# Turning neighbour means two blocks per q unit, and expert products in two PSUM banks: a graph layer with attention and routed experts

## The chip, the cores and the metric

The kernel runs on one core of a Trainium2 chip. The metric is the time of one execution on the device in microseconds (us). The kernel before takes 750.01 us, the median of 3 runs (749.41 to 750.44).

## What is computed

One layer of a graph transformer over 1,250 nodes of 512 values and 40,000 edges, sorted by destination. The three parts, cut to their core:

```python
xn = layernorm(x)
# graph part: mean of the neighbours' rows, two products, norm, relu
agg = segment_sum(xn[src], dst) / max(count(dst), 1)
gnn = relu(layernorm(xn @ w_self.T + agg @ w_neigh.T + bias) * gamma + beta)
# linear attention: 8 heads of 64, phi(t) = elu(t @ proj_mat) + 1
q, k, v = split(xn @ w_qkv)
kv = sum_n phi(k)[n] (x) v[n];  z = 1 / (phi(q) . sum_n phi(k)[n])
mix = (phi(q) @ kv * z) @ w_proj + b_proj
x = x + gnn + mix
# feed-forward: a shared hidden layer, and 2 of 8 experts per node
y = layernorm(x) * ln_scale + ln_bias
out = swiglu(y @ shared_in.T) @ shared_out.T + shared_out_b
h = swiglu(y @ expert_in.T)                  # one hidden row for all experts
for e in range(8): out += comb[:, e] * (h @ expert_out[e].T) + cnt[:, e] * bias[e]
return x + out
```

## The kernel before, in words

Each engine has a program of its own in `build`, written out in the order in which it is to run; semaphores (`S[...]`) tie the engines together. No scheduler moves anything: an instruction that waits holds up all that stands behind it on its engine. Every product of f32 values is made of three f16 products (high x high, high x low, low x high), in the helper `split3` (its matmul is L1343, so nearly all products carry that line). For a transposed operand this means: PE transposes a block into a PSUM bank, ACT copies it out as f16 (the high half), and DVE subtracts the high half from the bank and keeps the rest (the low half).

The change touches two stages.

**The q stage.** The sums of the neighbours lie in `aggacc`, ten blocks of 125 nodes. DVE makes means of them (L1029, one instruction per block, semaphore `an_rdy`). For each block, `means_T` then stands on three engines: PE transposes it (four matmuls, L1544, `aT_mm`), into bank 6 or 7 by turns, ACT writes the high half (L574, `aT_h`), DVE the low half (L1033, `aT_rdy`). PE may use the bank again when the low half of the block two before is made (L1542). Between the blocks PE makes the twelve q units: four pairs of heads for each of three groups of nodes (4, 4 and 2 tiles of 125 nodes), twelve matmuls each, in the banks `qb`. For each unit ACT makes two relus and an exponential (L585, L586, L588), and DVE adds up phi(q) (L1044, `q_rdy`). phi(q) is written to `qphi`, which is the same memory as `aggacc`, so a block has to be transposed before the q unit that writes over it. `MEANS` says which blocks PE turns after which q unit:

```python
MEANS = [(0, 1, 2), (3, 4, 5), (6, 7), (8, 9)] + [()] * 8
```

ACT has blocks 0 to 2 behind its unit 0 and blocks 3 to 9 behind its unit 1. DVE has all ten scalings first, then all ten low halves, and only then phi(q) of unit 0. `unit(U_PROJ)` converts a weight from f32 to two f16 halves: L435 on ACT and L745 on DVE. The attention tiles follow (`att`, L1572; the first of DVE's part at L1058 waits for all twelve `q_rdy`), then `att_turn` (L1581) and `project`.

**The expert stage.** The 2,500 pairs of node and expert are sorted by expert into tiles of 128 rows. GpSimd gathers the hidden rows of a tile (L377), PE turns them with 16 matmuls (`turn`, L1701) into the banks 4 to 7, ACT and DVE copy the turned rows out (L705, L1313; `hg_h`, `hg_l`). `expert` makes the product of a turned tile with the expert's weight, 24 matmuls of 512 columns, all in bank 0. ACT's `result` waits until it is done (`me_mm`) and until the store before has landed (`y_st`), copies bank 0 to `yb` (L710, `y_cp`), and issues the store to `y_rows` (L712). Pass i of PE's loop is: wait for `hg_h`, `hg_l`, `g_rdy`; turn tile i + 1; wait for `y_cp` of product i - 1; product i. Between experts ACT and DVE convert two weights each (`late_units`). Here there are 23 products. After them come ten tiles of the shared output (`so_mm`), in the banks `sobank`, and DVE adds the gathered expert rows and these banks to x (L1327, L1331).

Of the kernel before, what the change touches and what calls it, by code (L numbers as in the profile page):

```python
# [11 lines left out]
ACT = mybir.ActivationFunctionType  # L12
# [48 lines left out]
GROUPS = [(0, 4), (4, 4), (8, 2)]  # L61
MEANS = [(0, 1, 2), (3, 4, 5), (6, 7), (8, 9)] + [()] * 8
PARTS = [(0, 112), (112, P)]
# [27 lines left out]
def build(nc, a, out):  # L91
    with ExitStack() as ctx:
# [152 lines left out]
        kvb = [ps[3], ps[5]]  # L245
        qb = [ps[0], ps[1], ps[2], ps[4]]
        turned = [PS[:, 4 + 2 * z:6 + 2 * z, :].rearrange("p b (j n) -> p (b j) n", n=ST) for z in range(2)]

        sobank = [ps[i] for i in (1, 2, 3, 4, 5, 6, 7, 0)]

# [174 lines left out]
        def _(act):  # L425
# [145 lines left out]

            def means_T(b):
                act.wait_ge(S["aT_mm"], b + 1)
                s.activation(aggT[:, 0, :, b * BLK:(b + 1) * BLK], ps[6 + b % 2][:, 0:C * BLK].rearrange("p (c n) -> p c n", c=C),  # L574
                             ACT.Copy).then_inc(S["aT_h"], 1)
# [3 lines left out]
            for t0, nt in GROUPS:  # L579
                for r in range(PAIRS):  # L580
                    o, w = 1024 * (n % 2), nt * P
                    act.wait_ge(S["q_mm"], n + 1)
                    if n >= 2:
                        act.wait_ge(S["q_rdy"], n - 1)
                    s.activation(mscr[:, o:o + w], qb[n % 4][:, 0:w], ACT.Relu, scale=-1 / WS).then_inc(S["q_neg"], 1)  # L585
                    s.activation(mscr[:, o + 512:o + 512 + w], qb[n % 4][:, 0:w], ACT.Relu, scale=1 / WS).then_inc(S["q_rel"], 1)  # L586
                    act.wait_ge(S["q_neg"], n + 1)
                    s.activation(mscr[:, o:o + w], mscr[:, o:o + w], ACT.Exp, scale=-1.0).then_inc(S["q_exp"], 1)  # L588
                    for b in (range(3), range(3, NBLK))[n] if n < 2 else ():
                        means_T(b)  # L590
                    if n == 4:
                        unit(U_PROJ)
                    n += 1
# [113 lines left out]
            def result(i):  # L707
                act.wait_ge(S["me_mm"], i)
                act.wait_ge(S["y_st"], 16 * i)
                s.activation(yb, ps[0][:, :], ACT.Copy).then_inc(S["y_cp"], 1)  # L710
                act.wait_ge(S["y_cp"], i)
                act.dma_start(y_rows[bass.ds((i - 1) * ST, ST), :], yb).then_inc(S["y_st"], 16)  # L712
# [20 lines left out]
        def _(dve):  # L733
# [293 lines left out]
            link(v.reciprocal(cntacc[:, :], cntacc[:, :]))  # L1027
            for b in range(NBLK):
                v.tensor_scalar(aggacc[0:BLK, b, :], aggacc[0:BLK, b, :], cntacc[:, b:b + 1], None, ALU.mult).then_inc(S["an_rdy"], 1)  # L1029

            def means_T(b):
                dve.wait_ge(S["aT_h"], b + 1)
                v.tensor_tensor(aggT[:, 1, :, b * BLK:(b + 1) * BLK], ps[6 + b % 2][:, 0:C * BLK].rearrange("p (c n) -> p c n", c=C),  # L1033
                                aggT[:, 0, :, b * BLK:(b + 1) * BLK], ALU.subtract).then_inc(S["aT_rdy"], 1)


            for b in range(NBLK):
                means_T(b)
            n = 0
            for t0, nt in GROUPS:  # L1040
                for r in range(PAIRS):
                    o, w = 1024 * (n % 2), nt * P
                    dve.wait_ge(S["q_exp"], n + 1)
                    v.scalar_tensor_tensor(out=qphi[:, r, t0 * P:t0 * P + w], in0=mscr[:, o:o + w], scalar=1.0,  # L1044
                                           in1=mscr[:, o + 512:o + 512 + w], op0=ALU.mult, op1=ALU.add).then_inc(S["q_rdy"], 1)
                    n += 1
                    if n == 5:
                        unit(U_PROJ)
# [287 lines left out]
        def _(pe):  # L1336
# [201 lines left out]

            def means_T(b):
                pe.wait_ge(S["an_rdy"], b + 1)  # L1540
                if b >= 2:
                    pe.wait_ge(S["aT_rdy"], b - 1)  # L1542
                for c in range(C):
                    ins = te.transpose(ps[6 + b % 2][:, c * BLK:(c + 1) * BLK], aggacc[0:BLK, b, c * 128:(c + 1) * 128], ident[0:BLK, 0:BLK])  # L1544
                ins.then_inc(S["aT_mm"], 1)
# [166 lines left out]

            def expert(e, cur):
                split3(ps[0][:, :], lambda s, c: hgT2[:, cur(s * HID + c * 128)], unitv(U_EXP + 2 * e), J, True, True).then_inc(S["me_mm"], 1)

# [5 lines left out]
            pe.wait_ge(S["h_f"], 3 * J)  # L1721
            expert(0, lambda o: slice(o, o + 128))
            for e in range(EXP):
                pe.wait_ge(S["w_rdy"], U_EXP + 2 * e + 2)
                with pe.Fori(1 if e == 0 else ends[e - 1], ends[e]) as i:
# [4 lines left out]
                    turn(lambda o: hg2[:, bass.ds(nx + o, 128)])  # L1730
                    pe.wait_ge(S["y_cp"], i)
                    cur = pe.snap((i % 2) * ROWW)
                    expert(e, lambda o: bass.ds(cur + o, 128))

            pe.wait_ge(S["w_rdy"], U_SOUT + 2)
            pe.wait_ge(S["h_rdy"], 3 * J)
            for t in range(TILES):
                if t == 3:
                    pe.wait_ge(S["hg_h"], total + 1)
                    pe.wait_ge(S["hg_l"], total + 1)  # L1740
                if t == 7:
                    pe.wait_ge(S["y_cp"], total)
# [56 lines left out]
```

## Time and profile before

| | us |
|---|---|
| median of 3 runs | 750.01 (749.41 to 750.44) |
| the profiled execution | 746.69 |
| its span in the trace | 744.7 |
| PE matmuls busy | 708.5 (95%) |
| DVE busy | 386.4 (52%) |
| ACT busy | 261.9 (35%) |
| GpSimd busy | 174.4 (23%) |

The durations in the trace add up to the span; 2.0 us of the profiled execution lie around it. The profiled execution was 3.3 us shorter than the median of the runs. PE is TensorE's matmuls, PEld its weight loads, which run beside matmuls; the end of a matmul is modelled, so rows of matmuls overlap slightly, and a row's start is the more exact number. A name such as PEq or ACTq is the engine's sequencer. "[3.17 <-DVE big L1033]" behind a row of the timeline means that the engine stood idle for 3.17 us just before it and what released it.

### The profile page before, as it was taken

To read this page: it belongs to the slowest core of one execution; us is meant where nothing else is said; L and a number is where in the kernel's file an instruction comes from. 1 tells how busy PE (TensorE), PEld (TensorE's weight loads), DVE (VectorE), ACT (ScalarE), POOL (GpSimd) and SP (SyncE) were. 2 spreads that over 40 slices of the span, in tenths; PEclk is the share of its full clock that TensorE was granted. 3 is DMA by queue.
4 is the path that set the end of the run, shared out by engine and by line. 5 is a ranking of instruction groups with operands and counts; after the bars stand their busy time and mean duration, and the time that the engine had idled before them with its cause. 6 is when DMAs were issued, how large, how long until landed. Compare 5 with 4: busy or idle time off the path is not lost.

```text
span 744.7 us, 12041 instructions
## 1 busy us (share of the span) xinstructions
PE 708.5 (95%) x4382; PEld 433.8 (58%) x4382; DVE 386.4 (52%) x735; ACT 261.9 (35%) x386; POOL 174.4 (23%) x170
## 2 busy tenths in 40 slices
PE   6989899997999999998999999999889999999998
PEld 5646577774576656565756644446745555555554
DVE  5874678964476757876246422222235523441154
ACT  4853123323652231356353123333336443532000
POOL 3340000000061000013222257742312212222362
PEclk9999999998999999999999999999999999999999
DMA  9200002000031150011325212222166766643675
GB/s 249 96 1 1 1 2 114 2 13 2 1 138 61 29 198 1 0 28 28 114 84 169 56 28 58 58 79 92 29 227 239 264 216 239 230 136 130 195 211 150
DMA packets 24417, 73.90 MB, mean 99 GB/s; under 512 B 7059, under 2 KB 7405, under 8 KB 20274
## 3 DMA queue, kind: packets, MB, share of 16 engines
q1 hardware_dynamic: 8607, 39.74, 15.8%
q0 software_dynamic: 10768, 25.52, 11.6%
q10 hardware_dynamic: 4994, 8.01, 2.9%
q8 instruction: 31, 0.51, 0.3%
q14 instruction: 17, 0.13, 0.1%
HBM read 57.90 MB, written 15.31 MB: 98 GB/s over the span
## 4 chain that ended last, share of the span: by engine, by line
PE 77%; DVE 11%; ACT 6%; issue 3%; DMA 3%; DVEq 0%; POOL 0%; SPq 0%; ACTq 0%; POOLq 0%
PE banks L1343 59%; PE banks L1392 6%; PE banks L1380 3%; PE banks L1701 3%; DMA y_rows<-xT 2%; DVE st L768 1%; PE banks L1572 1%; PE banks L1366 1%; ACT W L435 1%; DMA x<-in_x 1%; PE banks L1581 1%; DVE xn L1154 1%; DVE W L745 1%; PE banks L1373 1%; ACT big L612 1%
## 5 line engine op out<-in xcount | busy, mean ns | idle before, releaser
L1343 PE MATMUL banks<-W,xT 128*125 128x512 f16 (+1 forms) x1392 | 318.2, 383 | 8.0 <-ACT xT L710 2.2
L1343 PEld LDWEIGHTS banks<-W,xT 128*125 128x125 f16 (+2 forms) x1392 | 165.3, 122 | 137.4 <-issue 15.9
L1343 PE MATMUL banks<-xT,W 128*128 128x500 f16 (+1 forms) x720 | 131.0, 344 | 1.8 <-DVE xn L1293 1.4
L1343 PEld LDWEIGHTS banks<-xT,W 128*128 128x128 f16 x720 | 70.7, 99 | 60.5 <-issue 4.4
L745 DVE SCALAR_TENSOR_TENSOR W<-stg,W 128x2048 f16<-128x2048 f32 x30 | 68.5, 2304 | 40.9 <-ACT W L435 40.9
L1343 PE MATMUL banks<-W,big 128*125 128x512 f16 x360 | 81.5, 380 | 0.0
L1343 PEld LDWEIGHTS banks<-W,big 128*125 128x125 f16 x360 | 48.3, 136 | 29.2 <-issue 2.3
L377 POOL DMA_INDIRECT xn<-h_rows,tokidx x29 | 35.3, 1217 | 125.1 <-PE banks L1701 114.7
L366 POOL TENSOR_TENSOR big<-xn,big 125x512 f16<-125x512 f32 x20 | 23.5, 1173 | 174.7 <-ACT big L627 174.7
L1313 DVE CAST xT<-banks 128x1024 f32 x22 | 26.9, 1222 | 69.0 <-PE banks L1701 69.0
L435 ACT ACTIVATE W<-stg 128x2048 f16<-128x2048 f32 x30 | 56.4, 1903 | 0.0
L1392 PE MATMUL banks<-W,big 125*125 125x512 f16 x200 | 54.0, 393 | 0.6 <-ACT big L566 0.6
L360 POOL TENSOR_TENSOR x<-x,bproj 125x512 f32<-125x512 f32 x10 | 14.4, 1476 | 165.6 <-DVE big L1044 165.6
L1293 DVE SCALAR_TENSOR_TENSOR xn<-banks,xn 128x500 f32<-128x500 f32 (+1 forms) x24 | 14.2, 591 | 69.8 <-ACT xn L689 69.8
L710 ACT ACTIVATE xT<-banks 128x512 f32<-128x512 f32 x23 | 13.7, 597 | 66.9 <-PE banks L1343 41.5
L390 POOL TENSOR_TENSOR big<-xn,big 128x500 f16<-128x500 f32 (+1 forms) x24 | 22.7, 945 | 45.9 <-ACT big L692 45.9
L689 ACT ACTIVATE xn<-banks 128x500 f32<-128x500 f32 (+1 forms) x24 | 12.4, 516 | 52.8 <-PE banks L1343 47.5
L897 DVE TENSOR_TENSOR W<-big 125x2048 f16<-125x2048 f16 x23 | 28.1, 1223 | 3.3 <-DVE big L893 2.4
L1154 DVE SCALAR_TENSOR_TENSOR xn<-banks,xn 125x512 f32<-125x512 f32 x20 | 13.8, 690 | 30.5 <-ACT xn L623 30.5
L1701 PEld LDWEIGHTS banks<-ident,xn 128*128 (+1 forms) x384 | 24.0, 100 | 8.5 <-issue 1.8
L1701 PE MATMUL banks<-ident,xn 128*128 128x128 f16 x384 | 26.2, 223 | 2.9 <-POOLq L382 1.5
L420 POOL DMA_INDIRECT xT<-y_rows,sloti x20 | 24.7, 1236 | 16.1 <-issue 9.3
(324 smaller groups left out, 785.0 us busy)
## 6 DMA issues: line engine op xcount, KB each, us to landing
stg<-in_units SPq DMA_DIRECT2D x30, 1024.0 KB
y_rows<-xT ACTq DMA_DIRECT2D x29, 256.0 KB
h_rows<-big POOLq DMA_DIRECT2D x10, 500.0 KB, 3.6
out_x<-x SPq DMA_DIRECT2D x10, 224.0 KB
stg<-in_wqkT SPq DMA_DIRECT2D x2, 1024.0 KB, 11.0
x<-in_x SPq DMA_DIRECT2D x2, 896.0 KB
xn<-h_rows,tokidx POOLq DMA_INDIRECT x29, 5.3
x<-in_x SPq DMA_DIRECT2D x1, 448.0 KB
```

The costliest lines, as they stand in the source:

```text
L366: g.tensor_tensor(hrow[t % 2][:, HID + 512 * u:HID + 512 * (u + 1)], mscr[0:P, 1024 + 512 * u:1536 + 512 * u], hrow[t % 2][:, 512 * u:512 ...
L377: g.indirect_dma_start(hg[i % 2], None, h_rows, bass.IndirectOffsetOnAxis(ap=tokidx[:, i:i + 1], axis=0)).then_inc(g_in[i % 2], 16)
L390: g.tensor_tensor(hT[:, 1, j, c0:c0 + w], mscr[:, 1024 + 512 * (n % 2):1024 + 512 * (n % 2) + w], hT[:, 0, j, c0:c0 + w], ALU.subtract).th ...
L420: g.indirect_dma_start(yg[n % 4], None, y_rows, bass.IndirectOffsetOnAxis(ap=sloti[:, 0, k, t:t + 1], axis=0)).then_inc(yg_in[n % 4], 16)
L435: s.activation(W[:, u % NSLOT, 0, :], stg[:, u % NSTG, :], ACT.Copy, scale=WS).then_inc(S["w_h"], 1)
L745: v.scalar_tensor_tensor(out=W[:, u % NSLOT, 1, :], in0=stg[:, u % NSTG, :], scalar=WS, in1=W[:, u % NSLOT, 0, :], op0=ALU.mult, op1=ALU.s ...
L897: return v.tensor_tensor(ohw[g % RING], iotaP.unsqueeze(1).to_broadcast(every), kr[g % KRING].rearrange("p k (a b) -> p (k a) b", b=2).uns ...
L1313: v.tensor_copy(hgT[:, bass.ds((i + 1) % 2, 1), 1].rearrange("p z j n -> p (z j) n"), turned[1]).then_inc(S["hg_l"], 1)
L1343: ins = te.matmul(dst, lhs(sl, c), rhs(sr, c), start=(first and c == 0 and k == 0), stop=(last and c == n - 1 and k == 2))
L1380: ins = te.matmul(ps[q][:, o:o + WK], ohw[z][:, CH // 2 + k // 2, :, k % 2], ohw[z][:, k // 2, 0:WK, k % 2], start=(h == 0 and k == 0), st ...
L1392: ins = te.matmul(ps[4 + z][0:BLK, :], CT[z][0:P, t, :], xs[:, s, t, :], start=(t == 0 and s == 0), stop=(t == TILES - 1 and s == 1))
L1701: ins = te.matmul(turned[s][:, j, :], rows(s * HID + j * 128), ident16[:, :], start=True, stop=True)
```

## The change

`MEANS` now gives each of the q units 0 to 4 two blocks, on PE, ACT and DVE alike. DVE scales four blocks first, and two more behind the low halves of each of the units 0, 1 and 2. `TURN_OF` is the order of the blocks (position p takes block `TURN_OF[p]`), such that each is turned before phi(q) is written over it. The conversion of `U_PROJ` stands behind q unit 6 on ACT and DVE, where it stood behind unit 4. The product of pass i goes to bank i % 2, by a register in the matmul's destination; PE no longer waits for `y_cp` in the loop; ACT reads bank (i + 1) % 2. `sobank` begins with bank 2, and the waits of the shared output move with it.

```diff
-MEANS = [(0, 1, 2), (3, 4, 5), (6, 7), (8, 9)] + [()] * 8
+MEANS = [(0, 1), (2, 3), (4, 5), (6, 7), (8, 9)] + [()] * 7
+TURN_OF = [0, 1, 2, 3, 4, 5, 7, 8, 6, 9]
...
+        PSflat = PS.rearrange("p b n -> p (b n)")
-        sobank = [ps[i] for i in (1, 2, 3, 4, 5, 6, 7, 0)]
+        sobank = [ps[i] for i in (2, 3, 4, 5, 6, 7, 0, 1)]
...
-            def means_T(b):
-                act.wait_ge(S["aT_mm"], b + 1)
-                s.activation(aggT[:, 0, :, b * BLK:(b + 1) * BLK], ps[6 + b % 2][:, 0:C * BLK].rearrange("p (c n) -> p c n", c=C),
+            def means_T(p):
+                b = TURN_OF[p]
+                act.wait_ge(S["aT_mm"], p + 1)
+                s.activation(aggT[:, 0, :, b * BLK:(b + 1) * BLK], ps[6 + p % 2][:, 0:C * BLK].rearrange("p (c n) -> p c n", c=C),
                              ACT.Copy).then_inc(S["aT_h"], 1)
...
-                    for b in (range(3), range(3, NBLK))[n] if n < 2 else ():
+                    for b in MEANS[n]:
                         means_T(b)
-                    if n == 4:
+                    if n == 6:
                         unit(U_PROJ)
...
-                s.activation(yb, ps[0][:, :], ACT.Copy).then_inc(S["y_cp"], 1)
+                s.activation(yb.unsqueeze(1), PS[:, bass.ds((i + 1) % 2, 1), :], ACT.Copy).then_inc(S["y_cp"], 1)
...
-            for b in range(NBLK):
+            def scale_mean(p):
+                b = TURN_OF[p]
                 v.tensor_scalar(aggacc[0:BLK, b, :], aggacc[0:BLK, b, :], cntacc[:, b:b + 1], None, ALU.mult).then_inc(S["an_rdy"], 1)
...
-            for b in range(NBLK):
-                means_T(b)
+            for b in range(4):
+                scale_mean(b)
             n = 0
             for t0, nt in GROUPS:
                 for r in range(PAIRS):
                     o, w = 1024 * (n % 2), nt * P
+                    for b in MEANS[n]:
+                        means_T(b)
+                    for b in MEANS[n + 2] if n < 3 else ():
+                        scale_mean(b)
                     dve.wait_ge(S["q_exp"], n + 1)
...
-                    if n == 5:
+                    if n == 7:
                         unit(U_PROJ)
...
-            def means_T(b):
-                pe.wait_ge(S["an_rdy"], b + 1)
-                if b >= 2:
-                    pe.wait_ge(S["aT_rdy"], b - 1)
+            def means_T(p):
+                b = TURN_OF[p]
+                pe.wait_ge(S["an_rdy"], p + 1)
+                if p >= 2:
+                    pe.wait_ge(S["aT_rdy"], p - 1)
                 for c in range(C):
-                    ins = te.transpose(ps[6 + b % 2][:, c * BLK:(c + 1) * BLK], aggacc[0:BLK, b, c * 128:(c + 1) * 128], ident[0:BLK, 0:BLK])
+                    ins = te.transpose(ps[6 + p % 2][:, c * BLK:(c + 1) * BLK], aggacc[0:BLK, b, c * 128:(c + 1) * 128], ident[0:BLK, 0:BLK])
...
-            def expert(e, cur):
-                split3(ps[0][:, :], lambda s, c: hgT2[:, cur(s * HID + c * 128)], unitv(U_EXP + 2 * e), J, True, True).then_inc(S["me_mm"], 1)
+            def expert(e, cur, bank):
+                split3(bank, lambda s, c: hgT2[:, cur(s * HID + c * 128)], unitv(U_EXP + 2 * e), J, True, True).then_inc(S["me_mm"], 1)
...
                     turn(lambda o: hg2[:, bass.ds(nx + o, 128)])
-                    pe.wait_ge(S["y_cp"], i)
                     cur = pe.snap((i % 2) * ROWW)
-                    expert(e, lambda o: bass.ds(cur + o, 128))
+                    bank = pe.snap((i % 2) * 512)
+                    expert(e, lambda o: bass.ds(cur + o, 128), PSflat[:, bass.ds(bank, 512)])
...
             for t in range(TILES):
-                if t == 3:
+                if t == 2:
                     pe.wait_ge(S["hg_h"], total + 1)
                     pe.wait_ge(S["hg_l"], total + 1)
-                if t == 7:
+                if t == 6:
                     pe.wait_ge(S["y_cp"], total)
```

The same at the places of the prediction, in the order of each engine. The low halves are the rows `big<-banks,big`, the scalings `big<-big,etabs`, phi(q) is `big<-xn`. DVE before, from the scalings on:

```order
L1029 TENSOR_SCALAR big<-big,etabs 125x512 [waits dve_ch]
L1029 TENSOR_SCALAR big<-big,etabs 125x512 x9
L1033 TENSOR_TENSOR big<-banks,big 128x4x125 [waits aT_h] x10
L1044 SCALAR_TENSOR_TENSOR big<-xn 128x500 [waits q_exp] x2
L1051 COPY kvbd<-banks 128x260 [waits kvacc_mm]
L1044 SCALAR_TENSOR_TENSOR big<-xn 128x500 [waits q_exp] x3
L745 SCALAR_TENSOR_TENSOR W<-stg,W 128x2048 [waits w_h]
```

DVE of the change, the same stretch up to unit 2:

```order
L1033 TENSOR_SCALAR big<-big,etabs 125x512 [waits dve_ch]
L1033 TENSOR_SCALAR big<-big,etabs 125x512 x3
L1038 TENSOR_TENSOR big<-banks,big 128x4x125 [waits aT_h] x2
L1033 TENSOR_SCALAR big<-big,etabs 125x512 x2
L1053 SCALAR_TENSOR_TENSOR big<-xn 128x500 [waits q_exp]
L1038 TENSOR_TENSOR big<-banks,big 128x4x125 [waits aT_h] x2
L1033 TENSOR_SCALAR big<-big,etabs 125x512 x2
L1053 SCALAR_TENSOR_TENSOR big<-xn 128x500 [waits q_exp]
L1060 COPY kvbd<-banks 128x260 [waits kvacc_mm]
```

The first low half stands behind four scalings where it stood behind ten, and phi(q) of unit 0 behind two low halves where it stood behind ten.

PE before, at the start of a pass's product in the expert loop (`banks<-ident,xn` is the turn, `banks<-W,xT` the product, ISA a register operation):

```order
L1701 ISA
L1701 MATMUL banks<-ident,xn 128x128
L1343 ISA [waits y_cp]
L1343 MATMUL banks<-W,xT 128x512 x2
L1343 ISA
L1343 MATMUL banks<-W,xT 128x512
```

PE of the change, the same place:

```order
L1711 ISA
L1711 MATMUL banks<-ident,xn 128x128
L1352 ISA
L1352 REGISTER_ALU
L1352 MATMUL banks<-W,xT 128x512 x2
L1352 ISA
L1352 MATMUL banks<-W,xT 128x512
```

The wait is gone, and one register operation per product is new, for the bank; the number of ISA rows between the matmuls is the same.

## Rows read from the trace of the kernel before

**Rows 1.** The page, part 1: busy time, share of the span, instructions.

```profile
PE 708.5 (95%) x4382; PEld 433.8 (58%) x4382; DVE 386.4 (52%) x735; ACT 261.9 (35%) x386; POOL 174.4 (23%) x170
```

**Rows 2.** Timeline of DVE in the tail: start, us, line, operation, count, [idle before <-releaser].

```profile
738.53 0.75 DVE L1327 SCALAR_TENSOR_TENSOR x<-xT,wch,x 125x512 f32<-125x512 f32 x1 [1.58 <-DMA xT<-y_rows,sloti]
741.28 0.69 DVE L1331 SCALAR_TENSOR_TENSOR x<-banks,x 125x512 f32<-125x512 f32 x1 [2.00 <-PE banks L1343]
```

**Rows 3.** Timeline of PE in the q stage (columns as in rows 2).

```profile
172.87 1.07 PE L1544 MATMUL banks<-ident,big 125*128 125x125 f32 x8 [0.22 <-DVE big L1029]
177.12 0.62 PE L1544 MATMUL banks<-ident,big 125*128 125x125 f32 x4 [3.17 <-DVE big L1033]
177.57 4.38 PE L1343 MATMUL banks<-xT,W 128*128 128x500 f16 x12
...
184.89 1.07 PE L1544 MATMUL banks<-ident,big 125*128 125x125 f32 x4 [2.09 <-DVE big L1033]
...
190.39 2.70 PE L1343 MATMUL banks<-xT,W 128*128 128x500 f16 x12
192.93 1.02 PE L1544 MATMUL banks<-ident,big 125*128 125x125 f32 x8
193.78 15.42 PE L1343 MATMUL banks<-xT,W 128*128 128x500 f16 x96
209.13 2.13 PE L1572 MATMUL banks<-kvbd,big 64*125 64x65 f32 x32
```

**Rows 4.** Stretches: length; busy us PE, PEld, DVE, ACT, POOL; granted clock; DMA share, GB/s.

```profile
172.80:177.10 4.30, 1.07 (x8) 0.86 (x9) 4.30 (x12) 2.42 (x5) 0.00 (x0) 1.00 0.01 2
177.10:182.00 4.90, 4.88 (x18) 2.33 (x19) 1.13 (x2) 0.61 (x2) 0.00 (x0) 0.65 0.00 0
```

**Rows 5.** Timeline of DVE in the q stage.

```profile
172.33 4.05 DVE L1029 TENSOR_SCALAR big<-big,etabs 125x512 f32<-125x512 f32 x10
176.30 1.25 DVE L1033 TENSOR_TENSOR big<-banks,big 128x500 f16<-128x500 f32 x2
...
210.46 0.42 DVE L1044 SCALAR_TENSOR_TENSOR big<-xn 128x250 f32<-128x250 f32 x1 [0.41 <-ACT xn L588]
```

**Rows 6.** Timeline of ACT in the q stage.

```profile
172.69 0.59 ACT L585 ACTIVATE xn<-banks 128x500 f32<-128x500 f32 x1 [7.77 <-PE banks L1343]
...
174.15 1.07 ACT L574 ACTIVATE big<-banks 128x500 f16<-128x500 f32 x2
```

**Rows 7.** Timeline of PE in the expert stage.

```profile
545.44 5.35 PE L1343 MATMUL banks<-W,xT 128*128 128x512 f16 x24
...
553.53 5.35 PE L1343 MATMUL banks<-W,xT 128*128 128x512 f16 x24 [1.85 <-ACT xT L710]
558.72 1.06 PE L1701 MATMUL banks<-ident,xn 128*128 128x128 f16 x16
559.79 5.35 PE L1343 MATMUL banks<-W,xT 128*128 128x512 f16 x24
...
679.02 5.35 PE L1343 MATMUL banks<-W,xT 128*128 128x512 f16 x24
```

**Rows 8.** Timeline of ACT and PE's weight loads in one pass of the expert loop.

```profile
559.01 0.60 ACT L710 ACTIVATE xT<-banks 128x512 f32<-128x512 f32 x1 [3.85 <-PE banks L1343]
559.78 4.86 PEld L1343 LDWEIGHTS banks<-W,xT 128*128 x24 [0.18 <-issue]
...
560.37 1.02 ACT L705 ACTIVATE xT<-banks 128x1024 f32 x1 [0.77 <-PE banks L1701]
561.29 3.70 ACT L435 ACTIVATE W<-stg 128x2048 f16<-128x2048 f32 x2
```

**Rows 9.** Timeline of ACT at the last product of the loop.

```profile
678.24 0.60 ACT L710 ACTIVATE xT<-banks 128x512 f32<-128x512 f32 x1 [3.87 <-PE banks L1343]
```

**Rows 10.** What ACT's copy of the product (L710) waited for: us, times.

```profile
  DMA y_rows<-xT: 25.3, 6
```

**Rows 11.** Register operations of the turn (L1701) on PE's sequencer: ns, starts.

```profile
L1701 PEldq FUSED_REGOPS  x352: 46/46/128, 540.9 to 677.4; - x176
```

More of the change, by code:

```diff
@@ L1027, in _ @@
             link(v.reciprocal(cntacc[:, :], cntacc[:, :]))
-            for b in range(NBLK):
+            def scale_mean(p):
+                b = TURN_OF[p]
                 v.tensor_scalar(aggacc[0:BLK, b, :], aggacc[0:BLK, b, :], cntacc[:, b:b + 1], None, ALU.mult).then_inc(S["an_rdy"], 1)
-            def means_T(b):
-                dve.wait_ge(S["aT_h"], b + 1)
-                v.tensor_tensor(aggT[:, 1, :, b * BLK:(b + 1) * BLK], ps[6 + b % 2][:, 0:C * BLK].rearrange("p (c n) -> p c n", c=C),
+            def means_T(p):
+                b = TURN_OF[p]
+                dve.wait_ge(S["aT_h"], p + 1)
+                v.tensor_tensor(aggT[:, 1, :, b * BLK:(b + 1) * BLK], ps[6 + p % 2][:, 0:C * BLK].rearrange("p (c n) -> p c n", c=C),
                                 aggT[:, 0, :, b * BLK:(b + 1) * BLK], ALU.subtract).then_inc(S["aT_rdy"], 1)
-            for b in range(NBLK):
-                means_T(b)
+            for b in range(4):
+                scale_mean(b)
             n = 0
@@ L1537, in _, with means_T @@
                 ins.then_inc(S["x_mm"], 1)
-            def means_T(b):
-                pe.wait_ge(S["an_rdy"], b + 1)
-                if b >= 2:
-                    pe.wait_ge(S["aT_rdy"], b - 1)
+            def means_T(p):
+                b = TURN_OF[p]
+                pe.wait_ge(S["an_rdy"], p + 1)
+                if p >= 2:
+                    pe.wait_ge(S["aT_rdy"], p - 1)
                 for c in range(C):
-                    ins = te.transpose(ps[6 + b % 2][:, c * BLK:(c + 1) * BLK], aggacc[0:BLK, b, c * 128:(c + 1) * 128], ident[0:BLK, 0:BLK])
+                    ins = te.transpose(ps[6 + p % 2][:, c * BLK:(c + 1) * BLK], aggacc[0:BLK, b, c * 128:(c + 1) * 128], ident[0:BLK, 0:BLK])
                 ins.then_inc(S["aT_mm"], 1)
@@ L1721, in _ @@
             pe.wait_ge(S["h_f"], 3 * J)
-            expert(0, lambda o: slice(o, o + 128))
+            expert(0, lambda o: slice(o, o + 128), ps[0][:, :])
             for e in range(EXP):
```

## The prediction

> **What bounds the kernel now.** The page's busy times come first: PE is busy 95% of the span, DVE 52%, ACT 35% [rows 1]. So an edit pays where PE stands still or runs slowly, or not at all. Next is the end of the kernel: DVE's last addition waits 2.00 us for PE's last tile, while the last gathered row was added 2.0 us before (738.53 + 0.75 against 741.28) [rows 2]. The end hangs on PE, and every us that PE wins earlier reaches it, as long as no other engine had less to spare.
>
> Then I looked in PE's timeline for places where it is not at full pace. In the q stage it waits 3.17 us and 2.09 us for DVE's low halves (L1033) [rows 3]. Both waits have a second price. The unit behind the first takes 4.38 us, the same twelve matmuls later take 2.70 us [rows 3]. The stretches tell why: PE is busy 1.07 of 4.30 us while it waits, and in the next 4.90 us, though it is busy throughout, the granted clock is 0.65 on average, that is partly 1.2 and partly 2.4 GHz [rows 4].
>
> Why the waits? DVE starts its ten scalings at 172.33 and needs 4.05 us for them; the first low half begins at 176.30 [rows 5]. But ACT had the first high half done by 174.15 + 0.59 = 174.74 [rows 6], so DVE came 1.6 us late. PE wants the third block turned before the second q unit, and it can't reuse a bank before that low half is made. Three blocks per unit in two banks make it worse: the third always waits for ACT and DVE.
>
> In the expert stage one wait is plain, 1.85 us at 553.53 [rows 7]. The others hide in the modelled ends of matmuls. Turn and product start at 558.72 and 559.79, 1.07 us apart [rows 7], and the weight loads stood idle for 0.18 us just before the product [rows 8]. ACT's copy of the last product ran from 559.01 to 559.61 [rows 8]; 0.18 us after its end the product starts. So the copy, not the array, sets the start of a product.
>
> **The change, part by part.**
>
> *q stage.* At full pace it needs: five pairs of transposed blocks at 0.85 us (192.93 to 193.78), three units at 2.54 us (190.39 to 192.93), and the last eight units at 15.35 us (193.78 to 209.13) [rows 3]. That is 4.25 + 7.62 + 15.35 = 27.22 us. It took 209.13 - 172.87 = 36.26 us. If nothing makes PE wait, **9.0 us** go: 5.3 us of waits, the rest the slow clock.
>
> Is the cover long enough? After a unit's start come 2.70 us until it ends [rows 3], 1.46 us of relus and exponential (172.69 to 174.15), 0.59 us for the first high half [rows 6], 1.25 us for two low halves [rows 5], and hops between engines, together some 0.2 us: 6.2 us. PE asks for the second of these banks after a unit, a pair, a unit and half a pair: 2.54 + 0.85 + 2.54 + 0.43 = 6.36 us. The margin is some 0.15 us. I take it as held, and note it as thin: a miss of 0.1 us in each of three units would cost 0.3 us and leave PE busy. DVE's own load for a unit is two low halves (1.25), two scalings (0.81), and phi(q), under 0.84 (a half-wide one takes 0.42) [rows 5]: at most 2.9 us in 3.39 us. The first pair of low halves waits for four scalings (1.6 us, to 173.95) and for ACT's 174.74, so the scalings are covered.
>
> The conversion of U_PROJ, now behind unit 6, takes ACT some 1.85 us (two take 3.70 [rows 8]) and is followed by five units, four of half width. Before, DVE's last phi(q) ended at 210.88 [rows 5], 1.75 us behind PE's last unit. By the same durations I get 1.7 to 2.0 us for it now, so the attention stage starts earlier by nearly the whole gain. Weights, bias and GpSimd's additions are released by events that move with it; I cost them at nothing.
>
> *Expert stage.* Without the wait for `y_cp` a pass is product plus turn: 5.19 us (553.53 to 558.72) and 1.07 - 0.18 = 0.89 us [rows 7, 8], 6.08 us in place of 6.26 us. From 545.44 to 679.02 there are 21 passes, 133.58 us; 21 x 6.08 = 127.68 us. With the 0.18 us ahead of the first one, **6.1 us** go: 3.9 us of the short waits and 2.2 us of the long ones.
>
> What takes over the duty of the wait is `hg_h`, which ACT signals behind the copy. In the pass shown it ends at 561.39 [rows 8], and PE wants it at the product's end, 564.98, so ACT has 3.4 us to spare in the shorter pass. The store that lands latest held ACT up by 1.85 us: covered. ACT's copy waited for a store 6 times of 23 [rows 10]; copy and issue take 0.78 us (559.01 to 559.79) [rows 7, 8], so a store may take 5.3 us before it sets the pass, and in the other 17 passes it had landed within 5.5 us. Late ones eat from the 3.4 us, and the next pass gives it back. In passes with two conversions ACT is busy until 564.99 [rows 8] and wanted at 565.07: still enough.
>
> The destination of the 24 matmuls is now in a register. No row prices this. PE's sequencer issues the last turn's register operations at 677.4 [rows 11] and next waits for ACT's copy, done at 678.84 [rows 9], so it is idle for 1.4 us of a pass of 6.26 and works 4.8 us. The lower bound is nothing, the upper one 128 ns per matmul, the longest of its register operations [rows 11]. I take nothing, since the order shows no further operation per matmul. Up to 52 ns per matmul (1.26 / 24) the idle time covers it.
>
> The Trainium skill ("TensorE: Matmul & The Clock Gate", section "Wait — 56ns, not 53.3ns?") says that matmuls are issued to the engine directly, and that through microcode each would take about 62 ns; it doesn't speak of register destinations, and no row here shows either price. By that figure, as an estimate, a pass would need 4.8 + 1.5 = 6.3 us, and the expert stage would give about 1 us.
>
> *Shared output.* The rotated banks move the waits of tiles 3 and 7 to tiles 2 and 6, 11 us or more behind the events that they wait for. Nothing.
>
> Sum: 9.0 + 6.1 = 15.1 us. Against the profiled execution that is 746.7 - 15.1 = 731.6 us; the median of the runs stands 3.3 us above it, so I forecast 750.0 - 15.1 = **734.9 us**.
>
> **The rivals.**
>
> *A. The short gaps are not the wait for the copy.* If the switch from turn to product costs 0.18 us by itself, only the long waits go: 133.58 - 21 x 6.26 = 2.1 us. Then 9.0 + 2.1 = 11.1 us, 738.9 us. Against it: the product follows the end of the copy by 0.18 us also when the copy is late, and the switch from product to turn costs nothing. The Trainium skill ("TensorE: Matmul & The Clock Gate", section "HAM oscillation — how this bites in real kernels") tells of a kernel to which PSUM double-buffering gave no further gain; by that rule A would be the outcome. The 0.18 us of idle weight loads in the row before [rows 8] speak against it, since a wait is there to be removed.
>
> *B. The chain through ACT and DVE is longer than summed.* If one wait of the size of the two stays, and with it the slow clock, half of the 9.0 us is lost: 739.4 us. For it: the thin margin. Against it: each engine's load per unit is below PE's.
>
> *C. Register destinations bind PE's sequencer.* At 128 ns per matmul a pass takes 4.8 + 3.1 = 7.9 us against 6.36 on average now: 21 x 1.5 = 32 us more, less 9.0 us: 773 us, slower than before. It turns the sign from 82 ns per matmul on ((6.36 + 9.0 / 21 - 4.8) / 24). Against it: the turn's weight loads have register addresses too, and run at full pace.
>
> *D. The gain is lost downstream* in a transfer or a chain that starts at a fixed time. I found none behind the q stage; the time would stay at 750 us.
>
> **How the numbers follow.** Forecast 0.75, A 0.12, B 0.07, C 0.04, D 0.02. The forecast's own range is about 732 to 738 us (the profiled execution and the median differ by 3.3 us, and so may two measurements). Up to 740.5 us it takes in A and B; C and D stay outside. A measurement of this kernel can tell about 0.2% (1.5 us) from no change. Faster 0.94, the same 0.02 (D), slower 0.04 (C).
>
> **What would show it.** Right: no wait above 0.3 us before the transposed blocks, a granted clock of 1.00 throughout the q stage, and the attention stage starting 27 us after the first transposition; product starts 6.08 us apart, no idle weight loads before a product, no PE wait for L710. Wrong: passes of 6.26 us (A), a wait for L1033's successor followed by slow units (B), passes above 6.3 us with idle weight loads between the product's matmuls (C), or a new wait of PE on another engine between the stages (D).

## The result and the profile after

The changed kernel takes 736.85 us (median of 4 runs, 735.89 to 738.54), the kernel before 750.23 us (median of 4). The ratio is 0.9852, with a 95% interval of 0.9819 to 0.9884: 13.4 us faster, where 15.1 us were forecast. Beside later runs of the kernel before it is 12.6 us (e5) and 12.4 us (e11). The profiled execution took 737.12 us, its span is 735.3 us. The page, part 1 (answers to [rows 1]):

```profile
PE 705.9 (96%) x4382; PEld 434.2 (59%) x4382; DVE 386.4 (53%) x735; ACT 261.8 (36%) x386; POOL 172.8 (23%) x170
```

Where did the time go? From the starts of the same instructions in both traces:

| stretch | before, us | after, us | difference |
|---|---|---|---|
| start to the first transposed block | 172.87 | 174.53 | +1.66 |
| to the first attention tile | 36.26 | 27.29 | -8.97 |
| to the second expert product | 336.31 | 336.09 | -0.22 |
| its 21 passes, to the last product | 133.58 | 131.67 | -1.91 |
| to the end | 65.68 | 65.72 | +0.04 |
| span | 744.7 | 735.3 | -9.4 |

The first line lies ahead of everything that was changed. Its 1.66 us are the clock, about (0.76 - 0.51) x 7.00 = 1.75 us: busy time in the stretch from 85 to 92 us (length; busy us and count of PE, PEld, DVE, ACT, POOL; granted clock, DMA share, GB/s), after, then before:

```profile
85.00:92.00 7.00, 7.00 (x23) 3.08 (x23) 4.68 (x13) 0.30 (x1) 0.00 (x0) 0.51 0.00 1
```

```profile
85.00:92.00 7.00, 7.00 (x45) 3.83 (x43) 5.26 (x13) 0.60 (x1) 0.00 (x0) 0.76 0.00 1
```

PE was busy all the time in both, at a granted clock of 0.51 and 0.76, with equal programs there. Such a difference is scatter between executions, and one execution cannot be set against another without looking for it.

**The q stage.** PE's timeline after (start, us, line, operation, count; answers to [rows 3]):

```profile
174.53 1.07 PE L1554 MATMUL banks<-ident,big 125*128 125x125 f32 x8 [0.22 <-DVE big L1033]
175.44 2.70 PE L1352 MATMUL banks<-xT,W 128*128 128x500 f16 x12
...
178.83 2.70 PE L1352 MATMUL banks<-xT,W 128*128 128x500 f16 x12
...
189.00 12.88 PE L1352 MATMUL banks<-xT,W 128*128 128x500 f16 x84
201.82 2.30 PE L1582 MATMUL banks<-kvbd,big 64*125 64x65 f32 x32
```

No wait stands behind the first one. A unit and a pair take 3.39 us (175.44 to 178.83), and the attention stage starts 27.29 us after the first transposed block; the forecast had 27.22. The granted clock is 1.00 from 172.80 to 204.00. DVE's timeline (answers to [rows 5]):

```profile
173.99 1.67 DVE L1033 TENSOR_SCALAR big<-big,etabs 125x512 f32<-125x512 f32 x4
176.44 1.26 DVE L1038 TENSOR_TENSOR big<-banks,big 128x500 f16<-128x500 f32 x2 [0.78 <-ACT big L577]
...
203.31 0.42 DVE L1053 SCALAR_TENSOR_TENSOR big<-xn 128x250 f32<-128x250 f32 x1 [0.41 <-ACT xn L591]
```

The scalings end at 175.66; the low half then waits 0.78 us for ACT, so the scalings are off the path. DVE's last phi(q) ends at 203.73, 1.9 us behind the start of attention; before it was 1.75 us.

**The expert stage.** PE's timeline (answers to [rows 7]):

```profile
537.91 5.34 PE L1352 MATMUL banks<-W,xT 128*128 128x512 f16 x24
543.09 1.06 PE L1711 MATMUL banks<-ident,xn 128*128 128x128 f16 x16
543.99 5.34 PE L1352 MATMUL banks<-W,xT 128*128 128x512 f16 x24
...
550.21 5.34 PE L1352 MATMUL banks<-W,xT 128*128 128x512 f16 x24
...
574.96 5.34 PE L1352 MATMUL banks<-W,xT 128*128 128x512 f16 x24
580.35 2.27 PE L1711 MATMUL banks<-ident,xn 128*128 128x128 f16 x16
582.67 5.34 PE L1352 MATMUL banks<-W,xT 128*128 128x512 f16 x24
587.91 2.16 PE L1711 MATMUL banks<-ident,xn 128*128 128x128 f16 x16
590.12 5.34 PE L1352 MATMUL banks<-W,xT 128*128 128x512 f16 x24
```

The first pass has 6.08 us (537.91 to 543.99), as forecast, with no gap between turn and product. But 543.99 to 550.21 is 6.22, and 574.96 to 582.67 is 7.71: the 16 matmuls of that turn took 2.27 us in place of 1.06 (both with 0.2 us of modelled end, so 0.13 to 0.14 us from start to start in place of 0.056 us). The next turn is nearly as slow, with 2.16 us. It isn't the clock, as the stretch around the first slow turn shows (columns as above):

```profile
577.50:584.30 6.80, 6.70 (x37) 3.41 (x36) 2.42 (x2) 5.71 (x5) 1.42 (x1) 1.00 0.38 135
```

Behind the first slow turn stands ACT:

```profile
569.67 0.34 ACTq L715 DMA_DIRECT2D y_rows<-xT  x1
...
577.69 0.60 ACT L713 ACTIVATE xT<-banks 128x512 f32 x1 [6.45 <-DMA y_rows<-xT]
...
579.02 1.02 ACT L708 ACTIVATE xT<-banks 128x1024 f32 x1 [0.73 <-ACT xT L713]
579.94 3.70 ACT L437 ACTIVATE W<-stg 128x2048 f16<-128x2048 f32 x2
```

The store issued at 569.67 held the next copy up until 577.69, 8.0 us later: ACT stood idle for 6.45 us. Not all of this is delay: in an undisturbed pass the copy starts 0.44 us behind the turn (601.81 and 601.37), here that would be 574.28, so it is 3.4 us late. The high half is done at 580.04, and the turn starts at 580.35. The second slow turn has DVE behind it, whose cast (`hg_l`) stands behind two conversions, which stand behind ACT's late ones:

```profile
581.88 4.49 DVE L748 SCALAR_TENSOR_TENSOR W<-stg,W 128x2048 f16<-128x2048 f32 x2 [5.53 <-ACT W L437]
586.29 1.22 DVE L1322 CAST xT<-banks 128x1024 f32 x1
```

The cast ends at 587.51, the turn starts at 587.91. What the copy waited for in all (answers to [rows 10]):

```profile
  DMA y_rows<-xT: 41.9, 12
  PE banks L1352: 23.2, 7
```

ACT stood idle until a store landed 12 times, before 6 times, and for 41.9 us in place of 25.3. These sums overstate the delay: ACT also idles some 3.6 us ahead of a copy that is on time, and in e4 below, where no copy waits for a store by itself, the same row reads 43.2 us in 10 times. The starts say more: counted as above, the copy began over 0.5 us late in 8 of the 22 passes of the loop, before in one.

### The profile page after: what moved, and what is told of

Read it like the earlier page. It is cut to its first block, busy times and chain, and to the rows that moved or that the text cites. A ratio compares the mean times of both kernels' runs of the same rounds, so it can differ in the third digit from the quotient of the medians.

```text
span 735.3 us, 12086 instructions
## 1 busy us (share of the span) xinstructions
PE 705.9 (96%) x4382; PEld 434.2 (59%) x4382; DVE 386.4 (53%) x735; ACT 261.8 (36%) x386; POOL 172.8 (23%) x170
## 4 chain that ended last, share of the span: by engine, by line
PE 82%; DVE 10%; ACT 4%; issue 3%; DMA 1%; DVEq 0%; POOL 0%; SPq 0%; ACTq 0%; POOLq 0%
PE banks L1352 62%; PE banks L1401 7%; PE banks L1711 3%; PE banks L1389 3%; DVE st L771 1%; PE banks L1582 1%; PE banks L1375 1%; DMA x<-in_x 1%; PE banks L1591 1%; ACT W L437 1%; DVE xn L1163 1%; PE banks L1382 1%; PE banks L1554 1%; PE banks L1416 1%; ACT big L615 1%
## 5 line engine op out<-in xcount | busy, mean ns | idle before, releaser
L1352 PE MATMUL banks<-xT,W 128*128 128x500 f16 (+1 forms) x720 | 128.3, 339 | 1.8 <-DVE xn L1302 1.4
L713 ACT ACTIVATE xT<-banks 128x512 f32 x23 | 13.7, 597 | 65.3 <-DMA y_rows<-xT 41.9
L1711 PE MATMUL banks<-ident,xn 128*128 128x128 f16 x384 | 28.6, 224 | 2.9 <-POOLq L384 1.5
L1711 PEld LDWEIGHTS banks<-ident,xn 128*128 (+1 forms) x384 | 25.3, 100 | 10.1 <-issue 2.7
L692 ACT ACTIVATE xn<-banks 128x500 f32<-128x500 f32 (+1 forms) x24 | 12.4, 516 | 52.7 <-PE banks L1352 47.5
L708 ACT ACTIVATE xT<-banks 128x1024 f32 x22 | 22.5, 1024 | 16.6 <-ACT xT L713 9.6
```

The source lines that it names most:

```text
L708: s.activation(hgT[:, bass.ds(i % 2, 1), 0].rearrange("p z j n -> p (z j) n"), turned[0], ACT.Copy).then_inc(S["hg_h"], 1)
L1352: ins = te.matmul(dst, lhs(sl, c), rhs(sr, c), start=(first and c == 0 and k == 0), stop=(last and c == n - 1 and k == 2))
L1711: ins = te.matmul(turned[s][:, j, :], rows(s * HID + j * 128), ident16[:, :], start=True, stop=True)
```

## The experiments

Two theories on the passes that stayed long. **Theory 1:** stores that share the DMA engines with two weight loads land late; ACT's copy, the conversions behind it and DVE's cast come late, and PE's turn is released when it should long have been issued. **Theory 2:** two banks or the register destination make passes long by themselves. Theory 1 leaves out a third signal that the turn waits for: `g_rdy`, that the gathered hidden rows of the next tile have landed. They come by DMA too, and share its engines with the same loads. Beside these: what in the q part counts, and what the medians have that the profiles don't. "Passes" is always the time from the start of the second product to that of the last. The kernel before ran with each group: median 746.99 us (17 runs, 741.64 to 751.71) beside e1 to e4, 748.00 (17 runs) beside e5 to e8, 748.34 (11 runs) beside e9 to e12.

**e1 and e2: each half alone.** e1 is the change without its expert part, e2 the kernel before with the expert part:

```diff
# e1, against the change
-    expert(e, lambda o: bass.ds(cur + o, 128), PSflat[:, bass.ds(bank, 512)])
+    pe.wait_ge(S["y_cp"], i)
+    expert(e, lambda o: bass.ds(cur + o, 128))        # bank 0
# e2, against the kernel before: the same two lines the other way round
```

> The q stage as in the change, the expert stage as before. If the q stage gives what its trace shows (27.3 us from the first transposed block to the attention stage, where it was 36.3), this is 9.0 us faster than before, about 741.2 us, ratio 0.988, and its expert passes are the 6.26 us of before. If part of the q gain is lost later (a fixed transfer, attention that waits), it is 745 us or more.

> The q stage as before, the expert stage as in the change. The forecast's 6.1 us would give 744.1 us. The trace of the change shows only 1.9 us won in the 21 passes, and the medians leave 4.4 us for this half, so I expect 746 to 748 us, with passes of 6.08 us and a few long ones around the weight loads. If the two halves disturb each other, this half alone gives the full 6.1 us.

e1: 736.83 us (6 runs), ratio 0.986 (0.982 to 0.990), 10.2 us faster. q stage 27.29 us, passes 133.70 us. e2: 744.94 us (12 runs), ratio 0.997 (0.9941 to 0.9999), 2.0 us faster. q stage 36.27 us, passes 131.56 us. So the q part makes most of the gain, the halves add up about (12.2 us) to what both give, and the expert part alone gives 2 us, not 6.1. Its ordinary passes are 6.07 us here too. Both came out below the expected times, and so did the kernel before beside them (746.99 us in place of 750.23). In e2 the longest of the 21 passes (7.68 us) wasn't a store's. ACT's high half was done at 590.36, 1.4 us ahead of the turn, and the cast earlier. But GpSimd's queue reported the gathered rows at 591.6, and the turn starts 0.2 us later:

```profile
L383 POOLq EVENT_SEMAPHORE  x1: 17/17/17, 591.6 to 591.6; - x1
```

```profile
591.78 2.18 PE L1702 MATMUL banks<-ident,xn 128*128 128x128 f16 x16
```

**e3: small loads.** It leaves out 15/16 of each weight from the fourth expert on (the shared output's too), and multiplies with older data there:

```diff
-    sp.dma_start(stg[:, u % NSTG, :], a["units"][u])
+    w = 2048 if u < U_EXP + 6 else 128
+    sp.dma_start(stg[:, u % NSTG, 0:w], a["units"][u][:, 0:w])
```

> The change, with 128 of 2048 columns loaded of the weights from the fourth expert on (the rest of the buffer keeps older weights). Theory 1 (stores of the products land late beside two weight loads, so ACT's copy, the conversions and DVE's cast come late, and PE's turn is released too late to be issued ahead): behind the third expert no copy waits for a store, those passes are 6.08 us, the 21 passes take under 129 us where the change took 131.7, and the time is 3 us or more below the change, under 734 us. Theory 2 (two banks or the register destination make passes long by themselves): the long passes stay, 131 to 132 us in all, and the time is that of the change.

731.00 us (4 runs). The passes take 127.54 us, all 21 of them 6.07 us. PE's timeline and ACT's, with the conversions in place:

```profile
560.86 5.34 PE L1353 MATMUL banks<-W,xT 128*128 128x512 f16 x24
566.04 1.06 PE L1712 MATMUL banks<-ident,xn 128*128 128x128 f16 x16
566.94 5.34 PE L1353 MATMUL banks<-W,xT 128*128 128x512 f16 x24
...
573.01 5.34 PE L1353 MATMUL banks<-W,xT 128*128 128x512 f16 x24
```

```profile
572.55 0.60 ACT L714 ACTIVATE xT<-banks 128x512 f32 x1 [3.73 <-PE banks L1353]
573.34 0.34 ACTq L716 DMA_DIRECT2D y_rows<-xT  x1
573.88 1.02 ACT L709 ACTIVATE xT<-banks 128x1024 f32 x1 [0.73 <-PE banks L1712]
574.80 3.70 ACT L438 ACTIVATE W<-stg 128x2048 f16<-128x2048 f32 x2
```

The passes from 560.86 to 573.01 are 6.08 and 6.07 us. No copy waits for a store, and ACT keeps up although it still makes its two conversions of 3.70 us. Theory 2 falls: banks and register destination are the same as in the change and cost nothing. The price of late transfers in the change is 131.67 - 127.54 = 4.1 us. That these are the stores alone, e3 can't say, since gathered rows land sooner with small loads as well. From 560 to 600 us the time from issue to landing was, for stores in e3, for stores in e4 (full loads), for gathers in e3, and for gathers in e2 (full loads):

```profile
DMA to landing us min/median/max: 2.0/2.0/2.4
```

```profile
DMA to landing us min/median/max: 2.0/4.7/6.8
```

```profile
DMA to landing us min/median/max: 4.3/4.4/6.0
```

```profile
DMA to landing us min/median/max: 4.3/7.5/10.9
```

So loads make both late.

**e4: two store buffers.** The copied product goes to one of two buffers, and the store is issued behind the high half. The wait for the store before stands just ahead of the issue, so that a buffer is free when its turn comes:

```diff
-    act.wait_ge(S["y_st"], 16 * i)                    # ahead of the copy
-    s.activation(yb..., PS[:, bass.ds((i + 1) % 2, 1), :], ACT.Copy)
-    act.dma_start(y_rows[...], yb)
-    high(i + 1)
+    s.activation(yb2[:, bass.ds((i + 1) % 2, 1), :], PS[:, bass.ds((i + 1) % 2, 1), :], ACT.Copy)
+    high(i + 1)
+    act.wait_ge(S["y_st"], 16 * i)                    # ahead of the store
+    act.dma_start(y_rows[...], yb2[(i + 1) % 2])
```

> The change with two buffers for the copied product, and the store issued behind ACT's high half, which then doesn't wait for the store before. A store may now take 6 us before it delays anything, and the high half never waits for one directly. Theory 1: the 21 passes take 128 to 129.5 us, no turn at the sequencer's pace, 2 to 4 us below the change, 733 to 735 us. Theory 2: no difference from the change, 736.9 us.

732.87 us (6 runs, 732.14 to 733.37), ratio 0.9803 (0.9768 to 0.9838). Passes 128.63 us: 19 of 6.07 or 6.08 us, one of 6.39 and one of 6.85. Loads, gathers and bytes stored are as in the change; only what a late store holds up differs. This shows theory 1 for most of the price: 3.0 us of the 4.1 (131.67 - 128.63). Buffer and place of the store were changed together, so neither's share is known. The pass of 6.85 us is still a late store's, by way of the conversions behind it:

```profile
635.96 3.71 ACT L439 ACTIVATE W<-stg 128x2048 f16<-128x2048 f32 x2 [1.42 <-DMA y_rows<-xT]
```

In the pass of 6.39 us the last signal ahead of the turn was that of the gathered rows.

**e5: the change again.**

> The change itself once more, on the same chip as the next three, for the comparison. q stage 27.3 us; the 21 passes between 130 and 133 us, as late stores fall; about 736.9 us.

735.43 us (6 runs), ratio 0.9837 (0.9795 to 0.9879); q stage 27.29 us, passes 132.31 us.

**e6: three blocks per unit, in DVE's new order.** The expert part is as before.

```diff
# against e1
-MEANS = [(0, 1), (2, 3), (4, 5), (6, 7), (8, 9)] + [()] * 7
+MEANS = [(0, 1, 2), (3, 4, 5), (6, 7), (8, 9)] + [()] * 8
-for b in range(4): scale_mean(b)
+for b in range(6): scale_mean(b)
```

> The q part alone, but with three, three, two and two blocks per unit as before; DVE's new order stays (six scalings ahead, low halves between the units). If DVE's ten scalings were what PE waited for, the stage takes the 27.3 us of the change. If two blocks for two banks are needed as well, the third block of units 0 and 1 still waits for relus, high and low half: about 1.7 and 2.1 us, 31 us in all, and up to 34 us if the slow clock comes with them.

PE's timeline:

```profile
175.74 0.62 PE L1553 MATMUL banks<-ident,big 125*128 125x125 f32 x4 [1.65 <-DVE big L1037]
176.19 2.70 PE L1351 MATMUL banks<-xT,W 128*128 128x500 f16 x12
...
181.83 0.62 PE L1553 MATMUL banks<-ident,big 125*128 125x125 f32 x4 [2.09 <-DVE big L1037]
...
204.41 2.29 PE L1581 MATMUL banks<-kvbd,big 64*125 64x65 f32 x32
```

The stage takes 31.40 us, with waits of 1.65 and 2.09 us and no slow clock. DVE's scalings off the path save 1.5 us of the first wait; the third block in two banks still waits for relus, high and low half, which two blocks per unit cure. The rest of the 4.9 us to the 36.26 us of before, some 3.3 us, is slow clock that this profile didn't have in the stage. The time didn't show the 4.9 us: 747.26 us (10 runs), ratio 0.9993 (0.9961 to 1.0026).

**e7: U_PROJ back behind unit 4.**

```diff
-    if n == 6: unit(U_PROJ)        # ACT; DVE: n == 7
+    if n == 4: unit(U_PROJ)        # ACT; DVE: n == 5
```

> The change with the conversion of U_PROJ back behind unit 4. The place costs nothing if ACT has room: by the durations ACT is busy 2.5 us of a pass of 3.4 us there, and 1.9 us more make it 1 us late for one unit, which the four q banks cover, so the q stage stays at 27.3 us and the time at that of the change. If the move was needed, the stage is 0.5 us or more longer, or DVE's last phi(q) comes earlier or later by over 0.5 us and takes the attention stage with it.

735.55 us (4 runs). The q stage has 27.29 us, the passes 129.56 us, and DVE's last phi(q) ends 1.5 us behind the start of attention (201.84):

```profile
202.93 0.42 DVE L1053 SCALAR_TENSOR_TENSOR big<-xn 128x250 f32<-128x250 f32 x1 [0.86 <-ACT xn L591]
```

In e5 it is 1.9 us. The place of the conversion is worth 0.4 us at most, and none that the times show.

**e8: two buffers, weights in four loads.** Against e4, each weight is loaded in four quarters of 2 KB per row.

```diff
-    sp.dma_start(stg[:, u % NSTG, :], a["units"][u])
+    for k in range(4):
+        sp.dma_start(stg[:, u % NSTG, 512 * k:512 * (k + 1)], a["units"][u][:, 512 * k:512 * (k + 1)])
```

> The kernel with two store buffers (store behind the high half), and each weight loaded in four quarters of 2 KB per row in place of rows of 8 KB. If the stores are late because their 2 KB rows alternate with longer rows of the loads, they land sooner beside a load, and the two long passes of 6.39 and 6.85 us go: 127.6 us for the 21 passes, 1 us less than with two buffers alone (732 us). If the four issues per weight or the shorter rows slow the loads, the conversions wait for weights and it is slower than 732.9 us.

735.41 us (6 runs), ratio 0.983: not better than e4. Passes 130.50 us. ACT's conversions now wait for weights (waits in the expert stage: total, times, longest):

```profile
ACT W L440 <- DMA stg<-in_units: 4.5, 3, 3.3
```

The pass behind the 3.3 us takes 8.10 us (570.80 to 578.90), and the one ahead of it, 6.88 us, had its gathered rows late. The expectation's second case came true. The first didn't: the last part of the stores issued at 558.4 and 564.5 landed 5.8 and 6.9 us later, no sooner than with whole loads (5.8 and 5.4 us for those of 556.6 and 563.3 in the change).

**e9 and e10: the kernels with waits in the q stage, profiled again.** e9 is the kernel before, e10 is e6.

> The kernel before, profiled once more. Its q stage takes 36.3 us again. If what is left of the difference between medians and profiles is the slow clock in the attention stage, which came in e1, e2 and e6 and not in the first profile of before, this profile may show it too (1.7 us or more from the attention stage to the first turned tile above 325.4 us); its passes take 133 to 135 us by late stores.

> The kernel with three blocks per unit once more. Theory S (scatter): its stage is 31.4 us again, 4.9 us below before, and what hid this in the time of e6 was 1.7 us of slow clock in the attention stage and long first passes; another profile may be without them. Rival: a stage with waits ahead of the attention stage always brings the slow clock there; then it shows again.

e9: 752.35 us, q stage 34.62 us, passes 136.28 us. e10: 748.53 us, q stage 33.06 us, passes 133.34 us. Both expectations, 36.3 and 31.4 us, missed. So the same waits bring two slow stretches, one or none: 34.62 and 36.26 us for the kernel before, 31.40 and 33.06 for three blocks. The attention stage had a slow stretch too, as the busy times in stretches show, of e9, then of the first profile of the same kernel (columns as above):

```profile
209.00:215.00 6.00, 5.33 (x59) 4.60 (x59) 4.32 (x16) 2.16 (x7) 4.12 (x4) 0.85 0.25 88
215.00:222.00 7.00, 7.00 (x43) 4.57 (x42) 5.55 (x8) 2.69 (x3) 7.00 (x5) 0.89 0.11 16
```

```profile
209.00:215.00 6.00, 5.33 (x63) 4.39 (x62) 4.62 (x17) 2.79 (x9) 3.98 (x4) 1.00 0.28 86
215.00:222.00 7.00, 7.00 (x58) 4.82 (x57) 5.88 (x9) 2.19 (x2) 7.00 (x5) 1.00 0.20 64
```

From the start of attention to the first turned tile the profiles take 325.1 to 325.5 us without such a stretch, 327.0 to 327.2 us (e1, e6, e9, e12) or 328.6 to 328.8 us (e2, e10) with it. It came in 4 of the 5 profiles of kernels that wait in the q stage, and in 2 of the 9 of kernels that don't. That would explain why the medians give the q part more than 9.0 us, and e6 nothing.

The span and mean granted clock on record for every run say more than 14 profiles. Span x (1 - clock) is an estimate of what ran below full speed, idle time in slow stretches included. Its means:

| kernel | span x (1 - clock), us |
|---|---|
| before (17, 17 and 11 runs) | 6.9, 8.7, 8.5 |
| e2, e6: waits in the q stage (12, 10 runs) | 7.7, 9.4 |
| the change (4 runs), e5, e11 (6 each) | 4.2, 4.3, 3.7 |
| e1, e4, e12 (6 runs each) | 4.8, 3.2, 5.6 |
| e3, e7 (4 runs each), e8 (6 runs) | 3.6, 5.0, 5.3 |

So the kernels that wait in the q stage run slower clocks over all their runs, and the three-block kernel no less than the kernel before beside it (9.4 and 8.7 us). Its 31.40 us came from a profile at a mean clock of 0.991, where its ten runs have 0.987. What is left, span x clock, has a mean of 735.7 us for e6 and 737.3 us for the kernel before, 1.6 us apart, as the 1.5 us of wait that e6 saves. It is an association: where the slow stretches of the other runs lay isn't known, and no run forced one.

**e11 and e12: the change and two store buffers side by side.**

> The change, side by side with two store buffers. 735 to 737 us; some turn of a tile follows a late store and is issued at the sequencer's pace; 21 passes in 130 to 133 us.

> Two store buffers and the store behind the high half, once more: 21 passes in 127.6 to 129.5 us, 2 to 4 us below the change of the same call, 732 to 734 us. If the gain of e4 was scatter, it is within 1 us of the change.

e11: 735.98 us (6 runs, 733.35 to 742.34), ratio 0.985 (0.9806 to 0.9895), passes 132.36 us. e12: 734.43 us (6 runs, 731.34 to 736.12), ratio 0.9808 (0.9769 to 0.9847), passes 128.38 us. The passes are 4.0 us shorter; e4's were 3.7 us shorter than e5's. Of the time 1.6 us are left here and 2.6 us from e5 to e4, less than the scatter of the runs, and the intervals overlap. So the time lies between the two cases of e12's expectation. Two store buffers are faster than the kernel before; their gain over the change is shown in the passes, not in the time. Where a part goes shows the tail of e12, PE, then DVE (answers to [rows 2]):

```profile
723.44 5.39 PE L1359 MATMUL banks<-W,big 128*125 128x512 f16 x24
```

```profile
729.36 0.75 DVE L1343 SCALAR_TENSOR_TENSOR x<-xT,wch,x 125x512 f32<-125x512 f32 x1 [0.88 <-DMA xT<-y_rows,sloti]
730.15 0.69 DVE L1347 SCALAR_TENSOR_TENSOR x<-banks,x 125x512 f32<-125x512 f32 x1
```

PE's last product ends at 728.83. DVE waits for gathered rows until 729.36, and its last addition at 730.15 doesn't wait for PE. The tail from the last product's start is 66.9 us, in the change 65.72: in this profile the gathers have become the end.

## Why the prediction was right, and where it was off

- **What bounds the kernel.** Right. Both halves took away PE's idle time, and the span fell by what PE won; the end hung on PE.
- **q stage, 9.0 us.** Right: 8.97 us in the first pair of profiles, 27.28 or 27.29 us in all nine profiles with two blocks per unit. The thin margin of 0.15 us held each time. But 9.0 us isn't a constant: against e9 it is 7.3 us, since the slow clock behind the waits comes in some executions twice, in some once. Of the 9.0 us, 5.3 us of waits are what the change takes away each time.
- **The 0.18 us before each product.** Right: they were the wait for the copy. Without it ordinary passes are 6.07 us (forecast 6.08). Rival A falls. The Trainium skill ("TensorE: Matmul & The Clock Gate", section "HAM oscillation — how this bites in real kernels") reports one kernel to which PSUM double-buffering gave no further gain. This kernel is not like it: two banks paid 0.18 us in each ordinary pass.
- **Expert stage, 6.1 us.** Mis-sized: 1.9 us in the first pair of profiles; over five profiles with the new expert part (the change, e2, e5, e7, e11) the passes average 131.5 us, over five with the old (before, e1, e6, e9, e10) 134.2 us, so 2.7 us. The term was summed as if every pass became ordinary, and the step that failed is "late ones eat from the 3.4 us, and the next pass gives it back". It looked at ACT's high half alone, and took a release just before the turn for early enough. First, the turn waits for three signals. DVE's cast waits behind two conversions, which wait behind ACT's, and the gathered rows come by DMA. DVE's timeline of the change in an undisturbed pass with conversions:

```profile
605.99 4.49 DVE L748 SCALAR_TENSOR_TENSOR W<-stg,W 128x2048 f16<-128x2048 f32 x2 [2.12 <-ACT W L437]
610.40 1.22 DVE L1322 CAST xT<-banks 128x1024 f32 x1
```

The cast ends at 611.62, and the turn that needs it starts at 613.52: 1.9 us ahead, not 3.4. Second, a turn that is released at the last moment is slow. In the nine profiles with two banks, 189 passes, the semaphore events show how long ahead of a turn's start the last of its three signals came, and how much the way from turn to product grew beyond 0.89 us:

| last signal ahead of the turn, us | turns | longer by, us |
|---|---|---|
| 1.75 or more | 139 | 0 |
| 1.5 to 1.75 | 11 | 0 to 0.22 |
| 1.0 to 1.5 | 26 | 0.02 to 0.50 |
| 0.5 to 1.0 | 5 | 0.71 to 1.13 |
| under 0.5 | 8 | 1.12 to 1.43 |

So a signal has to come some 1.5 to 1.75 us early. That leaves 0.2 to 0.4 us of cover for the cast behind conversions, and some 1.5 us for a high half that is done 3.2 us ahead (598.20 and 601.37). Against it, the copy came up to 3.4 us late. In the five profiles of the new expert part with one store buffer the passes lost 4.0 us each on average: 1.9 us where the cast came last, 1.15 us where the high half did, and 0.95 us where the gathered rows did. Lateness also adds up, where the forecast let the next pass give it back: the store of 569.67 was issued 1 us late itself, and so had 4.6 us to land, not 5.3.
- **Register destination: nothing.** Right. e3 has it and runs all passes at 6.07 us. Rival C falls. The Trainium skill ("TensorE: Matmul & The Clock Gate", section "Wait — 56ns, not 53.3ns?") gives about 62 ns per matmul through microcode. The pass of 6.3 us estimated from it didn't come. (It would have left 133.76 - 21 x 6.3 = 1.5 us, where the forecast says about 1.)
- **Rival B** (a remaining wait in the q stage) and **D** (lost downstream) didn't come. The total fits the forecast better than its parts, and that is luck: the medians give the q part 10.2 us alone (e1) where 9.0 were summed, which no term forecast, and the expert part 2.0 us (e2) where 6.1 were.
- **Reading of [rows 10].** "Waited for a store 6 times" counts a label. In three of the six the copy stood idle for 3.87 to 3.89 us, as it did with PE's label, and the next product came no more than 0.03 us late.

## What to carry to other kernels

If a wait is replaced by one that another signal covers, follow every engine that makes this signal, with all that is queued ahead of it, conversions, stores and gathers among them; the cover is the smallest of these, less the time that the sequencer needs to issue ahead (here 1.5 to 1.75 us for 16 short matmuls). Ask also which of the instructions on that path waits for a DMA: a transfer that shares its engines with bulk loads can be late, and it belongs behind the instruction that the critical engine waits for, with a second buffer (e4). And set profiles against each other stretch by stretch: here equal programs differed by 1.7 us ahead of the change.

## What the runs showed that wasn't expected

- A loop of short matmuls with register operations between them runs at 0.13 to 0.14 us per matmul when released late, and at 0.056 us when issued ahead; the profile shows this only as 2.27 us for 16 matmuls, without an idle time.
- The slow clock isn't a fixed part of a wait. The same program had granted clocks of 1.00 and 0.85 in the attention stage (windows above), and a q stage of 36.26 and 34.62 us.
- The kernel before scattered from 741.64 to 753.01 us in the 45 runs beside the experiments. The intervals here are 0.3 to 0.5% to either side, so the 0.2% that the forecast took for the least that could be told was too fine.
